# Routed expert loops rolled up: bodies of four parts, four places for gathered rows, gathers and scatters in groups of four

## The reference

```python
# layer 0: one expert, no biases
top1 = top_idx[:, 0]; w_top1 = weights[:, 0]
h = gelu(einsum('td,edh->teh', flat, W1)); y = einsum('teh,ehd->ted', h, W2)
out = w_top1[:, None] * y[token, top1]
# layer 1: two experts, biases; top_p are the two gates, divided by their sum
h = gelu(einsum('bsd,edh->bseh', x, w1) + b1)
expert_out = einsum('bseh,ehd->bsed', h, w2) + b2
return (top_p[..., None] * sel).sum(axis=2)
# layer 3: two experts, biases, relu; gate is zero but for the top two
h = relu(xf @ W1[e] + b1[e]); y = h @ W2[e] + b2[e]
out = out + gate[:, e:e + 1] * y
```

## Time and profile before

| | |
|---|---|
| median of 3 runs | 1601.01 us (1595.47 to 1602.18) |
| the profiled execution | 1609.27 us, span 1607.5 us |
| busy, PE / DVE / ACT / POOL | 1136.4 / 902.0 / 596.4 / 765.8 us |
| granted TensorE clock, mean over the span | 0.84 of full speed |
| f0, from first gather to last part | 102.2 to 219 us |
| f1, the same | 433.3 to 672 us |
| f3, the same | 1345.0 to 1584 us |

### The profile page before, as it was taken

How to read it: one execution, slowest core, us unless ns; L and a number is a source line. 1 busy time by engine, 2 the same in 40 slices (tenths; PEclk the granted TensorE clock), 3 DMA queues, 4 the chain that set the end, 5 groups by cost and what they waited for, 6 DMA issues and landing times. The chain is left out here.

```text
span 1607.5 us, 30375 instructions
## 1 busy us (share of the span) xinstructions
PE 1136.4 (71%) x8571; PEld 897.2 (56%) x8571; DVE 902.0 (56%) x2657; ACT 596.4 (37%) x1156; POOL 765.8 (48%) x872
## 2 busy tenths in 40 slices
PE   3534945992837778746767889996999775567793
PEld 2434943871537777634444455553888524467693
DVE  4651354567715456688874543346899534345484
ACT  2213635442314345534212223224445531334362
POOL 7143555664253554452435757864444104355543
PEclk8766977996759789979978999998999986687797
DMA  3051126000510111112113435531000023111115
GB/s 110 2 181 28 38 77 110 1 0 8 178 42 28 38 39 35 58 79 64 46 37 79 96 75 120 103 53 53 1 0 0 7 92 107 26 41 38 38 33 174
DMA packets 84777, 93.74 MB, mean 58 GB/s; under 512 B 18693, under 2 KB 65798, under 8 KB 83110
## 3 DMA queue, kind: packets, MB, share of 16 engines
q1 hardware_dynamic: 60278, 54.59, 11.6%
q0 software_dynamic: 21504, 30.08, 8.5%
q10 hardware_dynamic: 2864, 7.50, 1.2%
HBM read 64.31 MB, written 27.82 MB: 57 GB/s over the span
## 5 line engine op out<-in xcount | busy, mean ns | idle before, releaser
L1187 PE MATMUL psum<-f_xsT,f_w1e 128*128 128x128 f32 x1448 | 228.6, 308 | 143.6 <-ACT f_xsT L1231 96.0
L1187 PEld LDWEIGHTS psum<-f_xsT,f_w1e 128*128 128x128 f32 x1448 | 204.3, 218 | 160.1 <-issue 102.3
L1151 POOL DMA_INDIRECT d_y<-f_y,f_dst x160 | 156.4, 977 | 241.7 <-DVE f_y L1325 222.2
L1195 PE MATMUL psum<-f_w,f_hT 128*128 x1448 | 212.2, 293 | 16.4 <-issue 11.3
L1195 PEld LDWEIGHTS psum<-f_w,f_hT 128*128 128x128 f32 x1448 | 195.4, 209 | 18.0 <-issue 17.7
L1285 DVE TENSOR_TENSOR f_hpre<-psum,f_b 128x512 f32<-128x512 f32 x142 | 98.2, 692 | 122.7 <-remote 58.8
L1147 POOL DMA_INDIRECT f_xs<-d_xn,f_src x128 | 122.9, 960 | 92.6 <-POOLq L894 54.2
L1251 ACT ACTIVATE f_hT<-f_hpre 128x512 f32<-128x512 f32 x142 | 89.5, 630 | 196.7 <-DVE f_hpre L1285 143.9
L588 PE MATMUL psum<-ident,xn 128*128 128x128 f32 x256 | 46.9, 354 | 126.7 <-DVE xn L559 126.4
L2534 POOL DMA_INDIRECT d_acc<-f_y,f_token x64 | 100.8, 1575 | 50.0 <-DVE f_y L2863 32.3
L1241 ACT COPY f_w1e<-f_w 128x512 f32 x181 | 111.7, 618 | 15.9 <-issue 6.2
(11 more groups left out here) (476 smaller groups left out, 2422.4 us busy)
## 6 DMA issues: line engine op xcount, KB each, us to landing
f_w<-d_y SPq DMA_DIRECT2D x8, 1024.0 KB, 7.9
d_xn<-xn ACTq DMA_DIRECT2D x3, 2080.0 KB
f_w<-in_L_ffn_W SPq DMA_DIRECT2D x2, 2048.0 KB, 8.8
a_v<-in_ctx SPq DMA_DIRECT2D x4, 1024.0 KB, 14.6
f_wg<-in_WgT SPq DMA_DIRECT2D x16, 256.0 KB
f_wu<-in_WuT SPq DMA_DIRECT2D x16, 256.0 KB
f_wd<-in_WdT SPq DMA_DIRECT2D x16, 256.0 KB
d_y<-f_y,f_dst POOLq DMA_INDIRECT x160
```

What stands on the lines that cost most here:

```text
L1151: nc.gpsimd.indirect_dma_start(k.d_y, bass.IndirectOffsetOnAxis(m.dst[:, t:t + 1], 0), y[:, t % RY, :], None).then_inc(scattered[t % RY], 16)
L1187: last = nc.tensor.matmul(BH[n % 2][:, s * P:(s + 1) * P], w1e[:, u, s * P:(s + 1) * P], xsT[:, u, :], start=True, stop=True)
L1195: last = nc.tensor.matmul(BY[n % 2][:, 0:D], hT[:, n % RT, s, :], m.w2[:, bass.ds(e + s * D, D)], start=s == 0, stop=s == HS - 1)
```

## The change

`experts` no longer writes the parts out. PE, ACT and DVE each run a body of four parts: body 0 written out, bodies 1 to M/4 - 2 as a hardware loop with the number of the part in a register (DVE has two loops, since `y` places need clearing only from the eighth group on), and the last bodies written out. With that:

- `xs` has 4 places instead of 28, `y` 32 instead of 16, and turned tiles get 16 places in PSUM. Semaphores for gathers and scatters go from 28 + 16 to 4 + 4. POOL, still written out, issues four gathers and then the four scatters of the group five before. A gather into a place waits for its tile of the group before to be turned and for that group's gates to be kept.
- `turn_x(g)` stands four parts' time and more ahead of its group, at part 4g - 5 instead of 4g - 3.
- DVE reads one word (`m.pair`, with the numbers of parts n + 2 and n) at the head of each part, ahead of the bias. Gates are kept for four tiles at once (two 128x4 operations in f1 and f3, one in f0), and four places of `y` are cleared by one 128x512 copy of zeros in place of four memsets of 128x128.
- ACT reads the code right before it uses it, and copies x ahead of w.
- In a loop, each value that a semaphore is waited for is worked out from the loop's register.
- `route` makes `m.pair` with one more operation and a small copy.

```diff
-    RX, RY, RT = 28, SEG_RING, 4
+    RX, RY, RT, RP = TPC, SEG_RING, 4, 16          # SEG_RING 16 -> 32
+    LOOPED = M // TPC - 2
+    GY = RY // TPC
...
+        def fours(eng, body, cut=None):
+            body(0)
+            if cut is None or cut >= LOOPED:
+                with eng.Fori(1, LOOPED) as i:
+                    body(i)
+            else:
+                with eng.Fori(1, cut) as i:
+                    body(i)
+                with eng.Fori(cut, LOOPED) as i:
+                    body(i, True)
+            for i in range(LOOPED, (N + TPC - 1) // TPC):
+                body(i, True)
...
-                for t in range(RX):
-                    gather(t)
-                for t in range(M):
-                    if t + RX < M:
-                        pool.wait_ge(x_turned, t + 1)
-                        pool.wait_ge(gate_kept, t + 1)
-                        gather(t + RX)
-                    pool.wait_ge(y_ready, last_part(t) + 1)
-                    scatter(t)
+                BEHIND = 5
+                for g in range(M // TPC + BEHIND):
+                    for t in range(g * TPC, min((g + 1) * TPC, M)):
+                        if g:
+                            pool.wait_ge(x_turned, t - TPC + 1)
+                            pool.wait_ge(gates_kept, g)
+                        gather(t)
+                    for t in range(max((g - BEHIND) * TPC, 0), (g - BEHIND + 1) * TPC):
+                        pool.wait_ge(y_ready, last_part(t) + 1)
+                        scatter(t)
...
-                    if n % TPC == 1 and n - 1 + TPC < M:
-                        turn_x(n // TPC + 1)
+                            if u == 3 and within(i + 2, M // TPC):
+                                turn_x(i + 2)
...
+                def read_codes(n):
+                    pair = dve.value_load(m.pair[0:1, bass.ds(n, 1)], ...)
+                    return dve.snap((pair >> 12) & ((NE - 1) * HS)), dve.snap((pair >> 2) & ((NE - 1) * D)), dve.snap(pair & (RY - 1))
...
+                def keep_gates(g):
+                    for u in range(TPC):
+                        row_landed(dve, g, u)
+                    wait(dve, part_gated, TPC * g - TPC)
...
+                        nc.vector.tensor_tensor(gate_tmp[:], rows[:, :, D + 1], m.second[:, bass.ds(TPC * g, TPC)], ALU.mult).then_inc(gates_scaled, 1)
+                        dve.wait_ge(gates_scaled, g + 1)
+                        nc.vector.tensor_tensor(at, gate_tmp[:], rows[:, :, D], ALU.add).then_inc(gates_kept, 1)
+                def clear_y(g):
+                    for u in range(TPC):
+                        dve.wait_ge(scattered[u], 16 * (g - GY + 1))
+                    nc.vector.tensor_copy(..., bc(k.zeros[:, 0:D], (P, TPC, D), 1)).then_inc(y_cleared, 1)
...
+                def body(i, again=False):
+                    group = min(i, M // TPC - 1) if isinstance(i, int) else i
+                    for u in range(TPC):
+                        n = TPC * i + u
+                        if within(n, N):
+                            column, from_, slot = read_codes(n)
+                            if within(n + 2, N) and m.b1 is not None:
+                                bias(n + 2, u + 2, column)
+                            gate_part(n, u, group, slot)
+                            add_part(n, u, group, from_, slot)
...
+                            if u == 3 and within(i + 2, M // TPC):
+                                keep_gates(i + 2)
+                            if u == 2 and again and (not isinstance(i, int) or GY <= i + 1 < M // TPC):
+                                clear_y(i + 1)
```

More of the change, by code:

```diff
@@ L860, in route @@
     m.src = sb("src", [P, m.cols], I32) if m.choices == 2 else m.dst
-    m.expert, m.code = sb("expert", [1, N], I32), sb("code", [1, N], I32)
+    m.expert, m.code, m.pair = [sb(name, [1, N], I32) for name in ("expert", "code", "pair")]
     m.mine = sb("mine", [P, N])
@@ L1106, in tiles, with row_landed, within @@
             return slice(q * TP, (q + 1) * TP)
-        def code_of(eng, n):
-            code = eng.value_load(m.code[0:1, n:n + 1], min_val=0, max_val=(NE - 1) * FF + RY - 1)
-            return eng.snap(code & ((NE - 1) * FF)), eng.snap(code & (RY - 1))
         def last_part(t):
             return min(t + LATE, N - 1)
-        def landed(eng, sems, t):
-            eng.wait_ge(sems[t % len(sems)], 16 * (t // len(sems) + 1))
+        def row_landed(eng, g, u):
+            eng.wait_ge(gathered[u], 16 * (g + 1))
+        def fours(eng, body, cut=None):
[10 more added lines that the diff above has]
+                body(i, True)
+        def within(n, limit):
+            return not isinstance(n, int) or n < limit
         def add(eng, c, q):
@@ L1170, in expert_of, with turn_first, up_proj @@
                 def expert_of(n):
-                    return pe.value_load(m.expert[0:1, n:n + 1], min_val=0, max_val=(NE - 1) * FF)
+                    return pe.value_load(m.expert[0:1, bass.ds(n, 1)], min_val=0, max_val=(NE - 1) * FF)
                 def turn_x(g):
[L1175 to L1178, removed]
-                        nc.tensor.transpose(k.psum[:, t % RY * P:(t % RY + 1) * P], xs[:, t % RX, 0:D], k.ident[:]).then_inc(x_turned, 1)
-                def up_proj(n):
-                    u = n % RT
+                    if not isinstance(g, int) or g >= RP // TPC:
+                        pe.wait_ge(x_copied, g * TPC + TPC - RP + LATE)
+                    for u in range(TPC):
+                        row_landed(pe, g, u)
+                        nc.tensor.matmul(k.psum[:, bass.ds(((g & 3) * TPC + u) * P, P)], xs[:, u, 0:D], k.ident[:], start=True, stop=True).then_inc(x_turned, 1)
+                def turn_first(n):
+                    for t in range(n + 1):
+                        row_landed(pe, 0, t)
+                        nc.tensor.transpose(BY[n][:, t * P:(t + 1) * P], xs[:, t, 0:D], k.ident[:]).then_inc(first_turned, 1)
+                def up_proj(n, u):
                     pe.wait_ge(w_copied, n + 1)
@@ L1288, in keep_gate @@
-                def keep_gate(t):
-                    landed(dve, gathered, t)
-                    wait(dve, part_gated, last_part(t - RY) + 1 if t >= RY else 0)
-                    row, at = xs[:, t % RX], slot_gate[:, t % RY:t % RY + 1]
+                    nc.vector.tensor_tensor(hpre[:, u % 2], BH[u % 2][:].rearrange("p (s t) -> p s t", s=HS),
+                                            bc(m.b1[:, bass.ds(column, HS)], (P, HS, P), 2), ALU.add).then_inc(biased, 1)
+                def keep_gates(g):
+                    for u in range(TPC):
+                        row_landed(dve, g, u)
+                    wait(dve, part_gated, TPC * g - TPC)
+                    rows = xs[:]
+                    at = slot_gate[:, bass.ds((g & (GY - 1)) * TPC, TPC)]
@@ L1348, in measure @@
+                for g in range(GY):
+                    nc.vector.memset(y[:, g * TPC:(g + 1) * TPC, :], 0.0).then_inc(y_cleared, 1)
+                if m.b1 is not None:
+                    for n in range(2):
+                        e = dve.value_load(m.expert[0:1, n:n + 1], min_val=0, max_val=(NE - 1) * FF)
+                        bias(n, n, dve.snap(e >> 7))
+                keep_gates(0)
+                fours(dve, body, GY - 1)
                 def measure(q):
```

183 lines of the change are left out of this document (82 added, 101 removed).

## The result

The changed kernel takes 1703.59 us (median of 3, 1701.64 to 1706.06) against 1601.01: 1.065 times, 95% interval 1.061 to 1.070. It is slower by 103 us, where 86 us faster was forecast.

What follows compares the result with a forecast made beforehand. DVE was taken to bound f1 and f3 once holds go; f3 -38, f1 -38, f0 -19 and +2 made -93, giving 1516 us from the profiled execution, 1508 from the median. It took 1515, range 1490 to 1680.

Steps and rivals of the forecast that it cites:

- that the holds go: Premise for f0, f1 and f3: DVE's waits beside gathers, about 205 us of 595, vanish; forecast case at 0.49.
- The sign named for a wrong premise: Waits of 3 to 5 us ahead of bias or sum, put down to DMA or "remote", ending when the last of four gathers lands.
- f2 as a witness: In f2 POOL issues four gathers, then four scatter-adds of 1.62 us without pause, and no engine is held; support for the premise.
- The holds in f3's middle came with runs of gathers and scatters one by one.: Second support for the premise: f3's middle holds, 55 us or 1.6 us per gather, came with gathers and scatters issued singly.
- holds with each gather: Rival: each of 148 gathers between parts holds them 1.6 us, +237 us on -93; 1640 to 1740 us expected; chance 0.29.
- Start-up: Four gathers instead of 28 ahead of part 0, reached in 10 us; saves 32, 35 and 31 us in f3, f1, f0.
- DVE's part: DVE's time per part in f1 and f3 goes from 2.03 to 2.73 us, bounds 2.2 and 3.0.
- POOL: POOL's four gathers and four scatters take 10.1 us beside 10.9 us of four parts in f1 and f3; fits, barely.
- f0: Stage f0: 10 us to the first part plus 88 us of parts, partly paced by POOL; 98 against 116.8, -19 us.
- Loops: Hardware loops' branch costs once per four parts: 0.056 us on DVE, 0.215 us on PE, as in a1's loop.
- the fetch rival: Rival: instruction fetch at each of 5 + 13 + 13 loop turns on PE, +160 us, 1670 us; chance 0.06.

Runs made afterwards that it cites:

- e17: The kernel before with f2's scatter-adds made plain scatters (output not the reference's): 1602.42 us, against 1603.45 for the kernel before in the same call.
- e6: The changed kernel with only the first four gathers of each stage, scatters kept in groups of four (output not the reference's): 1531.89 us.
- e8: The changed kernel with scatters as plain DMAs of consecutive rows started by SP, so POOL only gathers (output not the reference's): 1576.96 us.

## Why the prediction was wrong

**The step that failed** is the premise that all of the sum was made to stand on: "that the holds go". Its case had 0.49. The holds stayed, at 6.5 us a turn. That is 1.6 per gather, the figure that was read from f3's middle before; since the price isn't one per gather, that it is the same figure is luck. The sign named for a wrong premise is what came, waits of 3 to 5 us put down to "remote", but they end with the landing of the last scatter and not of the last of four gathers.

- *f2 as a witness.* "It is the pattern that the change brings" took a scatter-add for a scatter. Its 1.62 us stood in the row next to 0.94, and with plain scatters in its place f2 is held too (e17). Nor did POOL keep its gap of 0.30 us throughout f2: up to 965 us it waited 5.5 to 7.1 us ahead of the adds of every second expert. A stretch that is free of a stall shows something only if the suspected cause is in it.
- *"The holds in f3's middle came with runs of gathers and scatters one by one."* They came with runs as such, of either kind or both (e6, e8). The change made the runs longer, from five or six to eight, and let them start in every group up to the last.
- *The rival that came true* is the first, holds with each gather, 1640 to 1740 us, at 0.29. Its time was right and its mechanism half right: it is a price of runs, not of gathers (e6 to e8), so its time was right in part by luck. The range left it at 1680, so it missed the time. With 0.29 in a case whose own range reached to 1740, the range was cut through the middle of that case.
- *Start-up.* Forecast 10 us to part 0, measured 12.6 to 13.5: some 28 us gained in each stage, as the sum has it, and given back with the gathers that moved between the parts.
- *DVE's part.* Forecast 10.9 us per four parts without holds (2.73 a part), 11.03 as made up above from parts that nothing holds. The load at the head of the part does what was said: 0.7 to 1.0 us of idle time ahead of a bias where there was none, and up to 1.4 behind the gates. The copy of zeros was 0.43 us for 0.5.
- *POOL.* The sum had its 10.1 us beside 10.9 us of parts. It is not beside them: four places tie its next run to the gates of the last group, and its run holds what those gates wait for. POOL's idle time of 7.2 us a turn shows it. The 28 places ahead let gathers go on while DVE was late; that they were worth having for it is read from the timelines, since no run has the groups of four with more places.
- *f0.* Forecast 98 us, 19 less than before; measured 126.8, 11 more, by the same holds: seven waits ahead of its scaled sum put down to "remote" are 37.8 us.
- *Loops.* Costing their branch at 0.056 us was right, and the fetch rival (0.06) fell with its reason: no fetches, no stall. What the loops cost, 18 to 26 us, is register work as far as the gaps ahead of the biases tell.

f3 can be made up from this: start-up -29 us; 56 parts at 0.73 us more than 2.03, +41; holds of 6.5 us in 13 turns, 85 instead of the 55 of before's middle, +30. That is +42 of the measured +48.

What stays open is the mechanism. Shown is that PE's matmuls are done and their signals come late, that this goes with a run of DMAs that POOL issues 1.3 us apart, that it grows faster than the run, and that pauses until the DMAs have landed shorten it. That the landing of the last one ends a hold fits the 20 turns above; in the start-up of the kernel before, though, the signals came 3.5 us after the last of 29 gathers had landed (1382.4 and 1385.9 us). A pause without a landing, the gather's and scatter's share in a run of other lengths, and a ring of eight places in the changed kernel, which would tell the length of the run from the tie between POOL and DVE, weren't tried.

## What to carry to other kernels

When a stall has no mechanism, its disappearance is not a premise for a sum: first pay for an experiment that makes it go, here a wait on POOL after every few gathers. Keep runs of indirect DMAs from one engine short while others work in step; in this kernel pauses after four gathers at the start and after six DMAs in the middle were worth 43 us, though each pause delays POOL. A ring of few places ties the engine that fills it to the slowest reader; count what happens when that reader is late, not only when all keep their pace.

## What was not expected of the hardware

- With a run of eight indirect DMAs on GpSimd (9.9 us from first to last), VectorE waited 3.6 us twice in a turn of 17.55 us for TensorE's matmuls, whose semaphores were updated up to 7 us after the modelled ends, several within 0.4 us; runs of four cost 1.6 to 2.4 us, runs of two hardly anything.
- In f2, four gathers and four scatter-adds of 1.6 us in a row don't do this; with plain scatters at 0.98 us in place of the adds they do, and it takes back the whole 2.4 us per expert that was saved.
- Plain DMAs in place of the gathers lower it (13.4 us a turn against 17.55), and 512 KB of other traffic for each tile doesn't (1728.94 us in all).
- TensorE's granted clock was 0.81 in the held loop and 1.00 in the 16 parts with gathers or scatters alone. In the turn shown it fell to 0.50, the lower of the levels 1.2 and 2.4 GHz, at 1513.6 us and rose again at 1520.4. Before the fall TensorE had been busy for 0.29, 0.35, 0.36 and 0.04 us in the four microseconds from 1508 on, and it stood still from 1512.9 to 1514.9. It isn't where the turn's 6.5 us go: those are the two waits, which lie at a clock of 1.00.
